# Mixture-of-experts stage: down weights loaded as two or three consecutive rows per partition, and the hidden products written in that order

## The chip, the cores and the metric

One Trainium2 chip, one of its cores. The metric is the device time of one launch in microseconds (us), as the median of the runs. A profiled execution has a time of its own, its span.

## What is computed

The program has three parts: a state-space kernel that makes 256 of the 384 tokens of each of 8 sequences, one attention layer, and a feed-forward layer with 64 experts. The change touches only the last one, here cut to what matters (T = 8 x 384 tokens, 512 wide, 64 experts, hidden width 352, at most 64 tokens for an expert):

```python
g = jnp.einsum('ech,ehi->eci', buf, w_gate)
u = jnp.einsum('ech,ehi->eci', buf, w_up)
y = jnp.einsum('eci,eih->ech', jax.nn.silu(g) * u, w_down)
out_slots = y[flat_i, slot] * (flat_w * valid)[:, None]
...
shared = jax.nn.silu(hidden_states @ sw_gate) * (hidden_states @ sw_up) @ sw_down
return y + shared
```

The last product sums over the 352 hidden values i of an expert. A sum may be taken in any order, so hidden values may stand in any order as long as the rows of `w_down` stand in the same one.

## The kernel before

All 64 experts run in `experts_phase` as 32 pairs (`PAIRS`), two experts of 64 tokens each on the 128 partitions. TensorE (PE) walks through a fixed order for each pair p: it turns the gathered token rows (L1793), multiplies them with the gate and up weights of both experts (L1803, 32 matmuls), turns the products of the hidden layer (`hm`, L1811, three transposes of 128, 128 and 96 columns) and multiplies those with the down weights (L1820, 12 matmuls). Between these four steps there are three gaps for each pair, and in 89 of the 96 gaps PE does a unit of the shared experts: `into_hidden` (L70, 12 matmuls) or `out_of_hidden` (L78, 18 matmuls). Fifteen units make one sequence. The gaps without a unit are gap 2 of pair 7, gap 1 of pair 15, gap 0 of pair 23, gap 2 of pair 30 and all three of pair 31. Gap 1 is the one between gate/up and the transposes of `hm`.

ScalarE (ACT) makes silu of the gate result (L1857). VectorE (DVE) multiplies it by the token's weight and the up result out of PSUM, into `hm` (L1933), copies the turned products back (`hmT`, L1939 and L1940), and copies the rows of y of the second expert (L1946); ACT copies those of the first (L1864). Both keep y in two buffers, and a copy waits until the adds of the pair two before have been done (`added`).

GpSimd (POOL) adds y to the output rows in memory: four indirect DMAs for each pair (L1958), two experts by two halves of the columns. Each waits until the add before it on the same half has landed, since rows may repeat between experts. The shared experts' result of a sequence is added in the same chain (L1966).

The weights come from SyncE (SP) into two sets of buffers, one for even and one for odd pairs. SP waits until gate/up of pair p-2 has been multiplied and issues the four gate and up loads of pair p (L111); then it waits until the down product of pair p-2 is done and issues the down loads of pair p (L118 and L120, two for each expert). A gate or up load takes four consecutive rows per partition, one run of 5,632 bytes. A down load takes rows of 2,048 bytes: chunk c, partition p holds row 128 c + p, and the third chunk has 96 rows. PE waits for all eight loads of a pair before L1803. The first two pairs are loaded by the same functions near the end of the attention part.

Of the kernel before, what the change touches and what calls it, by code (L numbers as in the profile page):

```python
# [11 lines left out]
ALU = mybir.AluOpType  # L12
ACT = mybir.ActivationFunctionType
AX = mybir.AxisListType
P = 128
# [95 lines left out]
            sp.dma_start(place[:, e, g], w[2 * p + e].rearrange("(p k) i -> p k i", p=P)).then_inc(done, 16)  # L111

def load_down(sp, place, w_down, p, done):
    I = w_down.shape[1]
    full = I // P
    for e in range(2):
        sp.dma_start(place[:, e, 0:full, :], w_down[2 * p + e][0:full * P, :].rearrange("(c p) d -> p c d", p=P))\  # L118
            .then_inc(done, 16)
        sp.dma_start(place[0:I - full * P, e, full, :], w_down[2 * p + e][full * P:I, :]).then_inc(done, 16)  # L120

def state_space_phase(nc, x, log_dt, B_ri, inv_A_real, A_imag, ident_in, h_dram, bulk, arena, late,
# [1525 lines left out]
def experts_phase(nc, acc, xrow, x2T_dram, slot_table, w_gate, w_up, w_down, bulk, shared, staged, added,  # L1649
                  late, rows_in, staged1):  # L1650

    E, D, I = w_gate.shape
# [32 lines left out]
    with ExitStack() as ctx:  # L1685
        def sb(name, shape, dt=F32):
            return ctx.enter_context(nc.sbuf_tensor(name, shape, dt))
# [9 lines left out]
        wcol = sb("mo_wcol", [P, 2])  # L1697
        scatter_half = sb("mo_scatter_half", [CAP, 2, E], U32)
        sil = sb("mo_sil", [P, I])
        hm = sb("mo_hm", [P, I])  # L1700
        hmT = sb("mo_hmT", [P, IC, P])
        y = sb("mo_y", [CAP, 2, 2, D])
        ps = ctx.enter_context(nc.psum_tensor("mo_ps", [P, 8, 512], F32))
# [49 lines left out]
        def _(pe):  # L1753
# [33 lines left out]
            for p in range(PAIRS):  # L1787
                j = p % 2
                use = p // 2 + 1
                pe.wait_ge(rows_in[p % 3], 16 * (p // 3 + 1))  # L1790
                wait(pe, rowsT_ready, p)
                for k in range(KC):
                    m = M.transpose(ps[:, 0, k * P:(k + 1) * P], xg[:, p % 3, k:D:KC], ident)  # L1793
                m.then_inc(rows_turned, 1)
                gap(p, 0)

                pe.wait_ge(rowsT_ready, p + 1)
                pe.wait_ge(w_in[j], 16 * 8 * use)
                wait(pe, hidden_ready, p)
                for g in range(2):  # L1800
                    for k in range(KC):
                        for e in range(2):
                            m = M.matmul(ps[CAP * e:CAP * (e + 1), 1 + g, 0:I], xgT[:, k, CAP * e:CAP * (e + 1)],  # L1803
                                         wgu[j][:, e, g, k, :], start=(k == 0), stop=(k == KC - 1))
                m.then_inc(gate_up_done, 1)
                gap(p, 1)

                pe.wait_ge(hidden_ready, p + 1)
                wait(pe, hiddenT_ready, p)
                for c in range(IC):  # L1810
                    m = M.transpose(ps[0:IW[c], 3, c * P:(c + 1) * P], hm[:, c * P:c * P + IW[c]], ident)  # L1811
                m.then_inc(hidden_turned, 1)
                gap(p, 2)

                pe.wait_ge(hiddenT_ready, p + 1)
                wait(pe, ya_ready, p)
                wait(pe, yb_ready, p)
                for c in range(IC):
                    for e in range(2):
                        m = M.matmul(ps[CAP * e:CAP * (e + 1), 4, :], hmT[0:IW[c], c, CAP * e:CAP * (e + 1)],  # L1820
                                     wd[j][0:IW[c], e, c, :], start=(c == 0), stop=(c == IC - 1))
                m.then_inc(down_done, 1)
# [44 lines left out]
        def _(dve):  # L1867
# [54 lines left out]
            for p in range(PAIRS):  # L1922
                j = p % 2
                dve.wait_ge(rows_turned, p + 1)
                wait(dve, gate_up_done, p)
                V.tensor_copy(xgT[:].rearrange("p k t -> p (k t)"), ps[:, 0, :]).then_inc(rowsT_ready, 1)  # L1926
                V.tensor_copy(wcol[0:CAP, j:j + 1], xg[0:CAP, p % 3, D + 2 * p:D + 2 * p + 1])
                V.tensor_copy(wcol[CAP:P, j:j + 1], xg[CAP:P, p % 3, D + 2 * p + 1:D + 2 * p + 2]).then_inc(wcol_ready, 1)
                after_unit(gap_units.get((p, 0)))
                dve.wait_ge(silu_done, p + 1)  # L1930
                dve.wait_ge(wcol_ready, p + 1)
                wait(dve, hidden_turned, p)
                V.scalar_tensor_tensor(out=hm[:], in0=sil[:], scalar=wcol[:, j:j + 1], in1=ps[:, 2, 0:I],  # L1933
                                       op0=ALU.mult, op1=ALU.mult).then_inc(hidden_ready, 1)
                if is_up(gap_units.get((p, 1))):
                    mult_shared(gap_units[p, 1])
                dve.wait_ge(hidden_turned, p + 1)
                wait(dve, down_done, p)
                V.tensor_copy(hmT[:, 0:IC - 1, :], ps[:, 3, 0:(IC - 1) * P].rearrange("p (c t) -> p c t", t=P))  # L1939
                V.tensor_copy(hmT[0:IW[-1], IC - 1, :], ps[0:IW[-1], 3, (IC - 1) * P:IC * P]).then_inc(hiddenT_ready, 1)  # L1940
                after_unit(gap_units.get((p, 1)), multiplied=True)
                after_unit(gap_units.get((p, 2)))
                dve.wait_ge(down_done, p + 1)
                for half in added:
                    wait(dve, half, 16 * (rank["pair", p - 2, 1] + 1) if p >= 2 else 0)
                V.tensor_copy(y[:, j, 1, :], ps[CAP:P, 4, :]).then_inc(yb_ready, 1)  # L1946
# [111 lines left out]
```

## Time and profile before

| | us |
|---|---|
| median of three runs | 1470.59 (1468.84 to 1477.54) |
| span of the profiled execution | 1472.2 |
| PE busy in it | 1291.1 |
| DVE busy | 754.7 |
| ACT busy | 407.8 |
| POOL busy | 499.0 |

The page cuts the span into 40 slices of 36.8 us. The experts' stage begins about 935 us from the start and takes the last 537 us. A line of the timeline is the start of a piece of work, its length, the engine, the line of the kernel and the tiles, and in brackets how long the engine was idle before it and what ended that. A line of the windows is a stretch of time with each engine's busy time and, at its end, the granted TensorE clock, the busy share of the DMA engines and the rate in GB/s.

### The profile page before, as it was taken

Reading aid. Unit: us, or ns where it says so; the run is one execution under the profiler, and the core shown is the slowest. Engines: PE = TensorE matmul, PEld = TensorE weight load, DVE = VectorE, ACT = ScalarE, POOL = GpSimd, SP = SyncE. Lnnn points to the kernel's source line nnn. Section 1 sums busy time; section 2 is a strip of 40 time slices with the busy share of each in tenths; the row PEclk is TensorE's granted clock in tenths of the full one; section 3 lists DMA queues with packets and bytes.
Section 4 is the critical chain, followed back from the end, with each engine's and each line's share of the span. In section 5 each row is a group of like instructions: output and inputs, shape, how many; then the busy total and the mean of one; then the engine's idle time right before and its main releaser. Section 6 shows DMA issues by size and latency. Waiting matters only on the chain. (4 is left out here: it accounts for less than half of the span.)

```text
span 1472.2 us, 23438 instructions
## 1 busy us (share of the span) xinstructions
PE 1291.1 (88%) x9192; PEld 823.0 (56%) x9192; DVE 754.7 (51%) x1666; ACT 407.8 (28%) x671; POOL 499.0 (34%) x453
## 2 busy tenths in 40 slices
PE   5196679999999999989887879999999999999995
PEld 5196434354545464636443668766666666665662
DVE  6984466567676777676765452222232322222321
ACT  2121313334434353444345341111111111111110
POOL 0000101011203434352456366243344444444444
PEclk9598759799999999999999989999999999999997
DMA  3024141221505152523242474699999999898983
GB/s 113 0 61 95 33 96 41 62 63 45 143 23 142 33 151 42 127 65 106 66 135 96 126 258 92 176 297 291 353 309 323 314 342 332 282 354 291 317 278 41
DMA packets 139829, 239.82 MB, mean 163 GB/s; under 512 B 61112, under 2 KB 81224, under 8 KB 139720
## 3 DMA queue, kind: packets, MB, share of 16 engines
q1 hardware_dynamic: 115880, 214.10, 45.6%
q0 software_dynamic: 23840, 24.23, 9.2%
q8 instruction: 73, 1.20, 0.3%
q14 instruction: 36, 0.29, 0.1%
HBM read 175.59 MB, written 38.90 MB: 146 GB/s over the span
## 5 line engine op out<-in xcount | busy, mean ns | idle before, releaser
L1958 POOL DMA_INDIRECT out_rows<-mo_y,mo_scatter_half x128 | 181.1, 1414 | 240.5 <-DMA out_rows<-mo_y,mo_scatter_half 171.6
L1322 DVE TENSOR_REDUCE late_view<-at_ps 128x1 f32<-128x384 f32 x384 | 195.3, 552 | 73.7 <-PE at_ps L893 65.0
L1098 ACT ACTIVATE bulk<-at_ps 128x1152 f32<-128x1152 f32 x128 | 144.6, 1130 | 280.9 <-PE at_ps L859 259.2
L1581 POOL DMA_INDIRECT slot_table<-at_toki,at_si x144 | 144.2, 1001 | 108.9 <-DVE late_view L1322 76.7
L70 PE MATMUL mo_ps<-arena_view,arena_view 128*117 128x384 f32 (+1 forms) x864 | 168.8, 344 | 1.1 <-PEq L549 1.1
L70 PEld LDWEIGHTS mo_ps<-arena_view,arena_view 128*117 128x117 f32 (+1 forms) x864 | 146.5, 179 | 14.6 <-issue 14.5
L893 PE MATMUL at_ps<-late_view 32*128 32x384 bf16 x384 | 102.2, 356 | 27.9 <-DVE late_view L1322 15.8
L850 PE MATMUL at_ps<-arena_view,arena_view 128*128 128x512 f32 (+1 forms) x576 | 115.7, 352 | 3.8 <-ACT arena_view L1176 2.4
L850 PEld LDWEIGHTS at_ps<-arena_view,arena_view 128*128 128x128 f32 x576 | 90.8, 194 | 37.3 <-issue 22.8
L893 PEld LDWEIGHTS at_ps<-late_view 32*128 32x128 bf16 x384 | 28.0, 92 | 142.8 <-DVE late_view L1322 103.4
L859 PE MATMUL at_ps<-arena_view 97*128 97x384 f32 x384 | 99.5, 369 | 8.6 <-DMA arena_view<-late_view 5.1
L1933 DVE SCALAR_TENSOR_TENSOR mo_hm<-mo_sil,mo_wcol,mo_ps 128x352 f32<-128x352 f32 x32 | 18.6, 580 | 155.9 <-ACT mo_sil L1857 141.0
L850 PE MATMUL at_ps<-late_view,late_view 128*128 128x512 f32 x288 | 91.5, 434 | 7.4 <-DVE at_hr L1355 5.3
L1553 POOL TENSOR_TENSOR arena_view<-arena_view,arena_view 128x640 f32<-128x640 f32 x24 | 37.3, 1556 | 173.5 <-DVE arena_view L1307 173.4
L1557 POOL TENSOR_TENSOR late_view<-arena_view,late_view 128x384 fp32r<-128x384 f32 x32 | 32.2, 1016 | 181.4 <-ACT late_view L1155 181.4
L485 PE MATMUL ss_psK<-arena_view,bulk 64*64 64x64 f32 x2048 | 61.9, 222 | 31.7 <-DVE bulk L431 31.7
L878 PE MATMUL at_ps<-bulk,at_ones 128*32 128x384 f32 x768 | 87.7, 531 | 1.2 <-issue 0.9
L878 PE MATMUL at_ps<-bulk,arena_view 128*32 128x384 f32 x768 | 86.2, 524 | 0.0
L859 PEld LDWEIGHTS at_ps<-arena_view 97*128 97x128 f32 x384 | 68.6, 199 | 29.5 <-issue 11.8
L78 PE MATMUL mo_ps<-arena_view,arena_view 117*128 117x512 f32 (+1 forms) x324 | 78.9, 397 | 4.8 <-DVE arena_view L1890 4.8
L1803 PE MATMUL mo_ps<-late_view,mo_xgT 128*64 128x352 f32 x512 | 79.3, 462 | 2.2 <-DVE mo_xgT L1926 2.2
L1803 PE MATMUL mo_ps<-bulk,mo_xgT 128*64 128x352 f32 x512 | 79.3, 462 | 1.1 <-DVE mo_xgT L1926 1.1
(216 smaller groups left out, 1812.0 us busy)
## 6 DMA issues: line engine op xcount, KB each, us to landing
bulk<-in_L_ffn_w_gate SPq DMA_DIRECT2D x32, 704.0 KB
bulk<-in_L_ffn_w_up SPq DMA_DIRECT2D x32, 704.0 KB
late_view<-in_L_ffn_w_gate SPq DMA_DIRECT2D x32, 704.0 KB
late_view<-in_L_ffn_w_up SPq DMA_DIRECT2D x32, 704.0 KB
arena_view<-arena_view SPq DMA_DIRECT2D x96, 192.0 KB
late_view<-in_L_ffn_w_down SPq DMA_DIRECT2D x32, 512.0 KB
bulk<-in_L_ffn_w_down SPq DMA_DIRECT2D x32, 512.0 KB
out_rows<-at_hr SPq DMA_DIRECT2D x8, 768.0 KB, 3.8
```

The source lines that it names most:

```text
L70: m = T.matmul(out, self.gu[:, wa, g, k, self.SO[c]:self.SO[c] + self.SW[c]], self.x2[:, xa, k, :], start=(n == 0), stop=(n == last))
L78: m = T.matmul(out, self.h[0:self.SW[c], xa, c, s * P:(s + 1) * P], self.d[0:self.SW[c], wa, c, :], start=(n == 0), stop=(n == last))
L485: m = T.matmul(psK[half, n % 2, i * STEP:(i + 1) * STEP], Pm[half, k % 2, t, h, :], basis, start=(t == 0), stop=(t == 3))
L850: m = T.matmul(out, xs[:, xa, k, x_cols], ws[:, wa, k, w_cols], start=(n == 0), stop=(n == 3 * KC - 1))
L859: m = T.matmul(ps[:, kt, 0:SEQ], QT[:, NH + h // REP, kt * P:(kt + 1) * P], QT[:, h, :], start=True, stop=True)
L878: m = T.matmul(ps[HD * j:HD * (j + 1), 3 + sums, 0:SEQ], w, PT[:, (REP * G + j) % RING, kt, :], start=(kt == 0), stop=(kt == NT - 1))
L893: T.matmul(ps[:, raw_bank(a, u), 0:SEQ], qb[rows, r, s * P:(s + 1) * P], qb[rows, REP, :], start=True, stop=True).then_inc(raw_scores, 1)
L1098: A.activation(PT[:, N % RING, :, :], ps[:, 0:NT, 0:SEQ], ACT.Exp, scale=float(HD) ** -0.5)\
L1322: V.tensor_reduce(maxes[:, half, s, h:h + 1], ps[:, raw_bank(a, u), 0:SEQ], AX.X, ALU.max, negate=True)\
L1581: G.indirect_dma_start(slot_table, bass.IndirectOffsetOnAxis(ap=si[:, e % 2, m:m + 1], axis=0), toki[:, e % 2, m // TOPK:m // TOPK + 1], N ...
L1803: m = M.matmul(ps[CAP * e:CAP * (e + 1), 1 + g, 0:I], xgT[:, k, CAP * e:CAP * (e + 1)], wgu[j][:, e, g, k, :], start=(k == 0), stop=(k == ...
L1958: G.indirect_dma_start(acc_halves, bass.IndirectOffsetOnAxis(ap=scatter_half[:, half, 2 * p + e:2 * p + e + 1], axis=0), y[:, p % 2, e, co ...
```

## The change

`load_down` gives partitions 0 to 95 three consecutive rows of `w_down` each (rows 3p to 3p+2, one run of 6,144 bytes) and partitions 96 to 127 two rows each (from row 288 on, one run of 4,096 bytes). There are still two loads for each expert, and as many bytes. Hidden value 3p+c then belongs to chunk c, partition p. So that the transposes of `hm` find the values of a chunk side by side, `hm` becomes three blocks of 128 columns, and DVE writes its products in that order, in two instructions: 288 values as 96 by 3 and 64 values as 32 by 2, read in sequence and written with a step of one block (512 bytes). PE and ACT do what they did.

```diff
+def down_rows(I):
+    IC = (I + P - 1) // P
+    wide = I - (IC - 1) * P
+    return IC, wide, IC * wide
 def load_down(sp, place, w_down, p, done):
-    I = w_down.shape[1]
-    full = I // P
+    IC, wide, split = down_rows(w_down.shape[1])
     for e in range(2):
-        sp.dma_start(place[:, e, 0:full, :], w_down[2 * p + e][0:full * P, :].rearrange("(c p) d -> p c d", p=P))\
+        sp.dma_start(place[0:wide, e], w_down[2 * p + e][0:split, :].rearrange("(p c) d -> p c d", c=IC))\
             .then_inc(done, 16)
-        sp.dma_start(place[0:I - full * P, e, full, :], w_down[2 * p + e][full * P:I, :]).then_inc(done, 16)
+        sp.dma_start(place[wide:P, e, 0:IC - 1, :],
+                     w_down[2 * p + e][split:, :].rearrange("(p c) d -> p c d", c=IC - 1)).then_inc(done, 16)
...
-        hm = sb("mo_hm", [P, I])
+        hm = sb("mo_hm", [P, IC, P])
...
-                    m = M.transpose(ps[0:IW[c], 3, c * P:(c + 1) * P], hm[:, c * P:c * P + IW[c]], ident)
+                    m = M.transpose(ps[0:IW[c], 3, c * P:(c + 1) * P], hm[:, c, 0:IW[c]], ident)
...
-                V.scalar_tensor_tensor(out=hm[:], in0=sil[:], scalar=wcol[:, j:j + 1], in1=ps[:, 2, 0:I],
-                                       op0=ALU.mult, op1=ALU.mult).then_inc(hidden_ready, 1)
+                _, wide, split = down_rows(I)
+                for first, last, c, rows in ((0, split, IC, slice(0, wide)), (split, I, IC - 1, slice(wide, P))):
+                    m = V.scalar_tensor_tensor(out=hm[:, 0:c, rows].rearrange("t c p -> t p c"),
+                                               in0=sil[:, first:last].rearrange("t (p c) -> t p c", c=c),
+                                               scalar=wcol[:, j:j + 1],
+                                               in1=ps[:, 2, first:last].rearrange("t (p c) -> t p c", c=c),
+                                               op0=ALU.mult, op1=ALU.mult)
+                m.then_inc(hidden_ready, 1)
```

On SP, in any pair of the stage, these rows stood before (the third number is the shape of one load, partitions first; `bulk` is the buffer of even pairs):

```order
L111 DMA bulk<-in_L_ffn_w_gate 128x1408
L111 DMA bulk<-in_L_ffn_w_up 128x1408
L118 DMA bulk<-in_L_ffn_w_down 128x2x512
L120 DMA bulk<-in_L_ffn_w_down 96x512
L118 DMA bulk<-in_L_ffn_w_down 128x2x512
L120 DMA bulk<-in_L_ffn_w_down 96x512
```

and these stand there now:

```order
L111 DMA bulk<-in_L_ffn_w_gate 128x1408
L111 DMA bulk<-in_L_ffn_w_up 128x1408
L125 DMA bulk<-in_L_ffn_w_down 96x1536
L127 DMA bulk<-in_L_ffn_w_down 32x1024
L125 DMA bulk<-in_L_ffn_w_down 96x1536
L127 DMA bulk<-in_L_ffn_w_down 32x1024
```

No load has moved in the queue; the number stays four, the shapes are other ones.

On DVE, in the pair after the one that ends a sequence, from the copy of the turned token rows to the copy of y, before:

```order
L1926 COPY mo_xgT<-mo_ps 128x512
L1927 COPY mo_wcol<-late_view_51 64x1
L1928 COPY mo_wcol<-late_view_51 64x1
L1933 SCALAR_TENSOR_TENSOR mo_hm<-mo_sil,mo_wcol,mo_ps 128x352
L1882 TENSOR_TENSOR arena_view_63<-arena_view_64,mo_ps 118x384
L1939 COPY mo_hmT<-mo_ps 128x256
L1940 COPY mo_hmT<-mo_ps 96x128
L1890 TENSOR_TENSOR arena_view_59<-arena_view_63,arena_view_59 118x384
L1946 COPY mo_y<-mo_ps 64x512
```

and now (the lines have moved down by 8, and by 14 behind the changed one):

```order
L1934 COPY mo_xgT<-mo_ps 128x512
L1935 COPY mo_wcol<-late_view_51 64x1
L1936 COPY mo_wcol<-late_view_51 64x1
L1943 SCALAR_TENSOR_TENSOR mo_hm<-mo_sil,mo_wcol,mo_ps 128x96x3
L1943 SCALAR_TENSOR_TENSOR mo_hm<-mo_sil,mo_wcol,mo_ps 128x32x2
L1890 TENSOR_TENSOR arena_view_63<-arena_view_64,mo_ps 118x384
L1953 COPY mo_hmT<-mo_ps 128x256
L1954 COPY mo_hmT<-mo_ps 96x128
L1898 TENSOR_TENSOR arena_view_59<-arena_view_63,arena_view_59 118x384
L1960 COPY mo_y<-mo_ps 64x512
```

One instruction has become two at the same place; everything behind it keeps its order.

## Rows read from the trace of the kernel before

**Rows 1.** The page: its head.
```profile
span 1472.2 us, 23438 instructions
```

**Rows 2.** Windows: stretch, its length, busy time of each engine, clock, DMA share, GB/s.
```profile
1375.00:1425.00 50.00, 48.38 (x273) 31.27 (x271) 14.35 (x32) 7.75 (x15) 20.46 (x16) 1.00 1.01 338
1425.00:1472.00 47.00, 29.51 (x146) 14.98 (x142) 7.55 (x17) 2.70 (x5) 22.58 (x16) 0.84 0.41 67
```

**Rows 3.** Waits of PE from 975 us on: us in total, times, longest.
```profile
PE mo_ps L1803 <- DVE mo_xgT L1926: 3.3, 3, 1.4
PE mo_ps L1811 <- DVE mo_hm L1933: 2.4, 2, 1.2
```

**Rows 4.** DMA issues of the even pairs' weights: loads, KB each.
```profile
bulk<-in_L_ffn_w_gate SPq DMA_DIRECT2D x32, 704.0 KB
bulk<-in_L_ffn_w_down SPq DMA_DIRECT2D x32, 512.0 KB
bulk<-in_L_ffn_w_down SPq DMA_DIRECT2D x32, 192.0 KB
```

**Rows 5.** Timeline of one pair around gap 1.
```profile
1204.53 2.34 PE L70 MATMUL mo_ps<-arena_view,arena_view 128*118 128x384 f32 x12
...
1205.14 0.58 DVE L1933 SCALAR_TENSOR_TENSOR mo_hm<-mo_sil,mo_wcol,mo_ps 128x352 f32<-128x352 f32 x1 [6.51 <-ACT mo_sil L1857]
...
1206.71 0.49 PE L1811 MATMUL mo_ps<-late_view,mo_hm 128*128 128x128 f32 x3
```

**Rows 6.** Timeline of PE where gap 1 has no unit.
```profile
1191.56 0.55 PE L1811 MATMUL mo_ps<-late_view,mo_hm 128*128 128x128 f32 x3 [1.18 <-DVE mo_hm L1933]
...
1452.20 0.55 PE L1811 MATMUL mo_ps<-late_view,mo_hm 128*128 128x128 f32 x3 [1.18 <-DVE mo_hm L1933]
```

**Rows 7.** Durations of DVE instructions, by line (mean or min/median/max, ns).
```profile
L1933 DVE SCALAR_TENSOR_TENSOR mo_hm<-mo_sil,mo_wcol,mo_ps 128x352 f32<-128x352 f32 x32 | 18.6, 580 | 155.9 <-ACT mo_sil L1857 141.0 <-issue 14.8
L1939 DVE COPY mo_hmT<-mo_ps 128x256 f32<-128x256 f32 x32 | 13.5, 422 | 42.6 <-PE mo_ps L1811 39.0 <-issue 3.6
L1940 DVE COPY mo_hmT<-mo_ps 96x128 f32<-96x128 f32 x32 | 8.9, 277 | 0.0
...
L351 DVE TENSOR_TENSOR arena_view<-ss_wt x5: 291/292/293, 26.6 to 30.8; 128x128 f32<-128x128 f32 x5
L351 DVE TENSOR_TENSOR late_view<-ss_wt x3: 393/400/402, 32.0 to 37.0; 128x128 f32<-128x128 f32 x3
```

**Rows 8.** Windows near the end: gate/up in flight, down in flight, nothing.
```profile
1419.00:1424.00 5.00, 4.42 (x20) 3.42 (x22) 0.45 (x2) 0.00 (x0) 1.74 (x2) 1.00 1.01 393
1429.00:1432.00 3.00, 3.00 (x15) 2.05 (x16) 0.47 (x1) 0.00 (x0) 1.24 (x1) 1.00 1.05 367
...
1425.20:1427.50 2.30, 2.30 (x14) 1.14 (x11) 0.74 (x2) 0.59 (x1) 1.55 (x2) 1.00 0.00 0
```

**Rows 9.** Chain that ended last: start, us, what; the gate/up of two pairs.
```profile
1395.36 4.88 PE mo_ps L1803 x32
...
1410.48 4.88 PE mo_ps L1803 x32
```

**Rows 10.** Timeline of POOL: adds beside down, beside gate/up, beside down.
```profile
1410.98 1.40 POOL L1958 DMA_INDIRECT out_rows<-mo_y,mo_scatter_half  x1 [4.69 <-DMA out_rows<-mo_y,mo_scatter_half]
...
1417.94 1.40 POOL L1958 DMA_INDIRECT out_rows<-mo_y,mo_scatter_half  x1 [3.85 <-DMA out_rows<-mo_y,mo_scatter_half]
...
1425.64 1.40 POOL L1958 DMA_INDIRECT out_rows<-mo_y,mo_scatter_half  x1 [4.60 <-DMA out_rows<-mo_y,mo_scatter_half]
...
1430.76 1.40 POOL L1958 DMA_INDIRECT out_rows<-mo_y,mo_scatter_half  x1 [2.02 <-DMA out_rows<-mo_y,mo_scatter_half]
```

**Rows 11.** Timeline of DVE and PE: a late copy of y, and waits.
```profile
1310.71 4.95 PE L1803 MATMUL mo_ps<-late_view,mo_xgT 128*64 128x352 f32 x32 [1.38 <-DVE mo_xgT L1926]
...
1325.49 0.69 DVE L1946 COPY mo_y<-mo_ps 64x512 f32<-64x512 f32 x1 [3.29 <-DMA out_rows<-mo_y,mo_scatter_half]
...
1326.96 4.95 PE L1803 MATMUL mo_ps<-bulk,mo_xgT 128*64 128x352 f32 x32 [1.06 <-DVE mo_xgT L1926]
```

## The prediction, made before the changed kernel ran

> **What bounds the kernel now.** I read the span and the windows first. The profiled execution took 1472.2 us [rows 1], 1.6 us more than the median of the runs, 1470.59. In a stretch of 50 us in the experts' stage PE is busy for 48.38 us at the full clock (granted share 1.00, its 2.4 GHz level) and the DMA engines' share is 1.01 at 338 GB/s; only the last 47 us look otherwise [rows 2]. So two resources stand at their limit there, and a change that makes the loads cheaper helps only if PE waits for loads. The waits of PE tell that it doesn't: in 497 us no wait on a DMA stands in that view. It waits 3.3 us for DVE's copy of the token rows and 2.4 us for DVE's products [rows 3]. The chain that ended last runs through PE from one gate/up to the next, 15.12 us for a pair with three L70 units (1410.48 - 1395.36) [rows 9]. Near the end one sees how early weights are: by 1425.2 the DMA engines stand still, so pair 31's gate and up weights have landed [rows 8]; its 4.9 us of products end 1.18 us before the transposes at 1452.20 [rows 6, 9], so they begin at about 1446, 20 us later. Down weights of a pair are issued when the down product two pairs before is done, and are needed at the gate/up of their own pair, more than 15 us later.
>
> There is a third chain, close behind PE: POOL's adds. One round is the adds of one expert. From the timeline: 1410.98 to 1417.94, 6.96 us, with down loads in flight for part of it; 1417.94 to 1425.64, 7.70 us, beside gate/up loads; 1425.64 to 1430.76, 5.12 us, beside down loads and a queue that had been empty [rows 10]. A pair costs POOL 6.96 + 7.70 = 14.66 us, and PE 15.12. The shared adds come on top, the longer pairs with L78 units give it back. Where the chain falls behind, DVE's copy of y waits for an add (3.29 us before the one at 1325.49), DVE is late with the next pair's token rows, and PE stands still: 1.38 us at 1310.71 and 1.06 us at 1326.96 [rows 11]. Those two are 2.44 of the 3.3 us. So loads reach PE's time by way of the adds, not by way of the weights.
>
> **The change part by part.** *Loads.* Their bytes stay: per pair 4 x 704 KB gate/up and 2 x (512 + 192) KB down [rows 4], 2.88 and 1.44 MB. Four issues stay four. Runs of down go from 2 KB (704 for a pair) to 6 and 4 KB (192 plus 64), 448 fewer. With gate/up in flight, runs of 5.6 KB, the rate was 393 GB/s, with down it was 367 [rows 8]. Both windows hold some adds as well, so the gain per pair is at most about 1.44 MB / 367 - 1.44 MB / 393 = 3.92 - 3.66 = 0.26 us, and it lies under PE. The weights were 15 us early: 0 on the path. All the gain could do is to shorten the adds' rounds.
>
> *Products on DVE.* The one instruction takes 580 ns for 352 values. Copies of 256 and 128 values take 422 and 277 ns, 1.13 ns for a value, so a fixed part of 580 - 352 x 1.13 = 182 ns [rows 7]. Two instructions take 182 + 288 x 1.13 = 507 and 182 + 64 x 1.13 = 254 ns. Consecutive DVE instructions overlap by about 80 ns (estimated from L1939 and L1940, which together end 0.62 us after the first began), so 681 ns: 0.10 us more. That is the lower bound. The writes now hop by 512 bytes at each value. No row has this hop; the nearest is L351, which writes 128 single values 32 bytes apart in 400 ns, against 292 ns side by side [rows 7], 0.84 ns more for a value. For 352 values that is 0.30 us, upper bound 0.10 + 0.30 = 0.40 us, which I take, as it is the nearest row. The Trainium skill (Vector Engine (DVE) Microarchitecture Reference, section Measured stream behaviour on trn2) says that a destination which hops at every element costs about 0.65 cycle more per element, at 0.96 GHz an estimate of 0.24 us for 352 values; by it the instructions would cost 0.34 us more. The row with its hop of 32 bytes is somewhat dearer, and the page says the same of small hops.
>
> What hides it: the L70 unit in gap 1. It starts at 1204.53 and runs 2.34 us, the products are ready at 1205.14 + 0.58 = 1205.72, and the transposes start at 1206.71 [rows 5]: 0.99 us of room against 0.40. Behind L1933 on DVE stand the shared product and the two copies of hmT; they wait for PE themselves. In two pairs, 15 and 31, gap 1 is empty, and PE waited 1.18 us in both [rows 6]. There the whole 0.40 us is paid: 0.8 us. PE's transposes read blocks of 128 columns as before, 0.
>
> **Sum.** 1472.2 + 0 (loads) + 0.8 = 1473.0 us for an execution like the profiled one; less the 1.6 us by which it lay above the median, 1471.4 us.
>
> **The rivals.**
> *The adds get shorter.* The saved 0.26 us of DMA time per pair is 1.3 us over the five pairs between two shared adds, and more if the 2 KB runs cost more beside adds than alone. That is the size of the stalls of 1.38 and 1.06 us. If both go: 1471.4 - 2.4 = 1469.0. For it: the margin of 15.12 - 14.66 us is thin. Against: these stalls occur in one of five sequences only, so there is nothing else to win.
> *The adds get longer, and the kernel slower.* An add's rows share the DMA engines with the loads. Beside loads of 5.6 KB a round takes 7.70 us, beside 2 KB loads 5.12 to 6.96 [rows 10]. If an add waits behind a number of runs and not of bytes, the new down loads of 6 KB make the second round as long as the first: 7.70 - 6.96 = 0.74 us more, 15.40 us for a pair, over PE's 15.12. The chain then falls behind by 0.28 us a pair on top of the margin it loses (0.46), so 0.74 x 5 = 3.7 us less is in reserve at the end of each sequence. The sequence with stalls would pay it all, the other four what exceeds their reserve; with 2 us of reserve in these (my estimate from there being no wait now) 3.7 + 4 x 1.7 = 10.5 us, and 1471.4 + 10.5 = 1482. With the 5.12 us round as the measure (7.70 - 5.12 = 2.58 us more a pair, 2.12 of them over the margin) it would be up to 30 x 2.12 = 64 us, 1535; but that round began with an empty queue, and new loads would find it as empty, so I keep it out of the range. It decides from 15.1 us for two rounds. The Trainium skill has the rule (DMA: Bandwidth & Descriptors, section Queues, rings and completion order): an engine goes round the queues by packets and drains some 9 to 17 descriptors of one before it turns to another. Rounds of 7.70 against 6.96 us agree with its direction. Against this rival: down runs go from 44 to 16 for each engine, so hardly more than one such batch is ever ahead, and the batch is 3.7 us at most.
> *Down loads become slow, and weights late.* Now two thirds of the partitions (0 to 63 of 96) take most of the first transfer, and the second one goes to 32 partitions. 
>
> **How the numbers follow.** Forecast, with or without a gain for the DMA engines, 0.60; shorter adds 0.22; longer adds 0.12; slow down loads 0.03; something else 0.03. About 1% (14.7 us) is what a measurement of this kernel can tell from no change. Within it lie the forecast, the shorter adds and over half of the longer adds; slower by more: 0.05 + 0.03 + 0.01; faster by more needs a gain that no wait of PE offers, 0.02. The forecast's own range is 1470.6 (DVE at its lower bound, 0.2 us: 1470.8, and a little less) to 1473. The range of 8 in 10 reaches down to the shorter adds less the runs' own scatter (the lowest run was 1.8 us under the median), 1467, and up into the longer adds, 1480; the highest run of before, 1477.54, lies inside.
>
> **What would show it.** Right: L1943 as 64 instructions, the two of a pair together about 1.0 us; PE's wait before the transposes of pairs 15 and 31 about 1.6 instead of 1.18 us, and in no other pair; no wait of PE on a DMA; a similar or lower DMA share at the same PE time; fewer packets on the page, by about 14,300. The adds decide the rest: two rounds of POOL well under 14.7 us and no wait at the places of 1310.71 and 1326.96 speak for the shorter adds; rounds beside down near 7.7 us, more waits of ACT's and DVE's copies of y on an add, and waits of PE on the token rows in each sequence speak for the longer ones. Wrong would be: PE waiting before L1811 for anything but DVE (weights late), or the products so slow that the 0.99 us of gap 1 is used up, which would need more than 1.6 us for the two.

## The result, and the profile after

The changed kernel takes 1512.72 us (median of 5 runs, 1507.5 to 1521.89) against 1470.59 us for the kernel before (5 runs, 1467.23 to 1477.54). The ratio is 1.0268 with a 95% interval of 1.0231 to 1.0306: 2.7% slower, far outside the predicted range. (Ratios here and below are taken over undisturbed executions alone, so they can differ a little from the quotient of two medians; the profiled execution of e5, with 1521.98 us the longest of its six, is not among them.)

The head of the page of after, and the waits of PE from 975 us on (in total, times, longest). The lines of before stand 8 to 14 further down: gate/up L1803 is now L1811, the transposes L1811 are L1819, DVE's products L1933 are L1943, the copy of the token rows L1926 is L1934, DVE's copy of y L1946 is L1960, the pair adds L1958 are L1972.

```profile
span 1520.0 us, 23470 instructions
PE 1291.4 (85%) x9192; PEld 823.4 (54%) x9192; DVE 766.0 (50%) x1698; ACT 407.9 (27%) x671; POOL 501.3 (33%) x453
PE mo_ps L1811 <- DVE mo_xgT L1934: 52.0, 7, 13.3
PE mo_ps L1819 <- DVE mo_hm L1943: 2.9, 2, 1.5
```

Against [rows 1, 3] PE waits 48.7 us more for DVE's copy of the token rows and 0.5 us more for the products. It still waits for no DMA of weights. The experts' stage runs from the first gate/up to the end: 1472.2 - 940.05 = 532.2 us before and 1520.0 - 931.63 = 588.4 us after.

```profile
940.05 4.95 PE L1803 MATMUL mo_ps<-bulk,mo_xgT 128*64 128x352 f32 x32
```
```profile
931.63 4.95 PE L1811 MATMUL mo_ps<-bulk,mo_xgT 128*64 128x352 f32 x32
```

(The stage happened to start 8.4 us earlier in this execution; in the kernels below the start of the stage moves by some 10 us, without order.) Of the 56.2 us, 49.2 are those waits. The rest is PE's clock. Behind each of the four long stalls (10.16, 13.29, 13.12 and 11.22 us) the granted share falls from 1.00, its 2.4 GHz level, to the 1.2 GHz one for a while. The windows (stretch, length, busy time of PE, PEld, DVE, ACT, POOL, granted clock, DMA share, GB/s) that hold a long stall show it below 1, the ones between at 1:

```profile
1125.00:1175.00 50.00, 39.84 (x212) 25.21 (x210) 12.02 (x28) 5.63 (x11) 23.58 (x18) 0.90 0.81 235
1175.00:1225.00 50.00, 46.08 (x255) 29.49 (x251) 12.76 (x27) 7.05 (x12) 13.94 (x10) 1.00 1.05 310
1225.00:1275.00 50.00, 39.18 (x216) 24.56 (x217) 13.00 (x30) 6.14 (x12) 22.27 (x17) 0.86 0.88 252
```

The timeline of PE shows a gate/up group behind a stall and the next one. The first runs at a lower clock for part of its time, 2.2 us longer. The four groups behind the four stalls lose 2.2, 1.7, 1.6 and 2.9 us, 8.3 together. Before had lost 1.7 us in the same way at its very last down product, which after doesn't, so 7 us remain.

```profile
1139.19 7.16 PE L1811 MATMUL mo_ps<-bulk,mo_xgT 128*64 128x352 f32 x32 [10.16 <-DVE mo_xgT L1934]
...
1156.53 4.95 PE L1811 MATMUL mo_ps<-late_view,mo_xgT 128*64 128x352 f32 x32
```

**What is late.** The waits of all engines name it:

```profile
DVE mo_y L1960 <- DMA out_rows<-mo_y,mo_scatter_half: 75.0, 7, 17.9
POOL out_rows L1972 <- DMA out_rows<-arena_view: 58.7, 10, 10.2
```

Before, these were

```profile
DVE mo_y L1946 <- DMA out_rows<-mo_y,mo_scatter_half: 10.9, 6, 3.3
POOL out_rows L1958 <- DMA out_rows<-arena_view: 29.3, 10, 4.5
```

In time order, one stall on POOL, DVE and PE:

```profile
1207.96 1.52 POOL L1972 DMA_INDIRECT out_rows<-mo_y,mo_scatter_half  x1 [10.19 <-DMA out_rows<-arena_view]
1216.26 1.46 POOL L1972 DMA_INDIRECT out_rows<-mo_y,mo_scatter_half  x1 [6.78 <-DMA out_rows<-arena_view]
```
```profile
1234.35 0.69 DVE L1960 COPY mo_y<-mo_ps 64x512 f32<-64x512 f32 x1 [17.94 <-DMA out_rows<-mo_y,mo_scatter_half]
1235.08 0.69 DVE L1934 COPY mo_xgT<-mo_ps 128x512 f32<-128x512 f32 x1
```
```profile
1235.82 4.56 PE L1811 MATMUL mo_ps<-late_view,mo_xgT 128*64 128x352 f32 x18 [13.29 <-DVE mo_xgT L1934]
```

The two adds of the shared rows hold POOL's chain for 17 us, the pair adds behind them are late, DVE's copy of y may not overwrite its buffer for 17.94 us, the copy of the next token rows stands behind it, and PE has nothing to multiply. That is the chain of [rows 11], with a wait of PE ten times as long. It comes in each sequence: in the first PE waits only 1.07 and 2.28 us, in the four others 10 to 13. The rounds of the pair adds in one pair picked as in [rows 10] are:

```profile
1371.10 1.42 POOL L1972 DMA_INDIRECT out_rows<-mo_y,mo_scatter_half  x1 [6.15 <-DMA out_rows<-mo_y,mo_scatter_half]
...
1378.64 1.39 POOL L1972 DMA_INDIRECT out_rows<-mo_y,mo_scatter_half  x1 [4.43 <-DMA out_rows<-mo_y,mo_scatter_half]
...
1388.95 1.42 POOL L1972 DMA_INDIRECT out_rows<-mo_y,mo_scatter_half  x1 [5.91 <-DMA out_rows<-mo_y,mo_scatter_half]
```

7.54 us beside gate/up as before, but 10.31 us beside the new down loads, 17.85 us for this pair against 14.66 before and PE's 15.12. (Means over the stage follow behind the table.)

**Why the adds are late.** A stretch of 3 us in which only down loads and adds are in flight, as the 367 GB/s of [rows 8], and the landing times of the page, which stand at the end of an issue's row:

```profile
1399.50:1402.50 3.00, 3.00 (x21) 1.61 (x21) 1.11 (x2) 0.52 (x1) 0.19 (x1) 1.00 1.08 301
1478.00:1481.00 3.00, 3.00 (x16) 2.13 (x16) 0.31 (x1) 0.00 (x0) 0.66 (x1) 1.00 1.03 299
...
bulk<-in_L_ffn_w_gate SPq DMA_DIRECT2D x32, 704.0 KB, 7.4
bulk<-in_L_ffn_w_down SPq DMA_DIRECT2D x32, 576.0 KB, 7.8
```

The DMA engines are as taken as before and move 300 instead of 367 GB/s: 1.44 MB take 4.8 instead of 3.9 us, 0.9 us more for a pair. Counted over every microsecond of the stage in which no gate/up load was in flight and down loads took most of the engines' time, the mean rate is 314 GB/s before and 258 after. A transfer of 576 KB lands 7.8 us after its issue, one of 704 KB for gate after 7.4. The packets' own durations in the trace say the same (medians): 84 ns for 2 KB before; after, 378 ns for 6 KB and 264 ns for 4 KB. The 5.6 KB packets of gate/up stay at 215. The loads of the shared experts' turned token rows (x2T below) come in 6 KB packets over 128 partitions, and those took 234 in before. So it is not the length of a run that is slow. Which transfers are, the experiments asked.

### The profile page after: what moved, and what is told of

Same layout as the page of the kernel before. It is cut to its first block and busy times, and to the rows that moved or that the text cites. A ratio compares the mean times of both kernels' runs of the same rounds, so it can differ in the third digit from the quotient of the medians.

```text
span 1520.0 us, 23470 instructions
## 1 busy us (share of the span) xinstructions
PE 1291.4 (85%) x9192; PEld 823.4 (54%) x9192; DVE 766.0 (50%) x1698; ACT 407.9 (27%) x671; POOL 501.3 (33%) x453
## 2 busy tenths in 40 slices
DMA packets 125493, 239.82 MB, mean 158 GB/s; under 512 B 61112, under 2 KB 81224, under 8 KB 125384
## 5 line engine op out<-in xcount | busy, mean ns | idle before, releaser
L1972 POOL DMA_INDIRECT out_rows<-mo_y,mo_scatter_half x128 | 182.3, 1424 | 297.0 <-DMA out_rows<-mo_y,mo_scatter_half 198.7
L70 PEld LDWEIGHTS mo_ps<-arena_view,arena_view 128*117 128x117 f32 (+1 forms) x864 | 146.5, 179 | 14.6 <-issue 14.5
L901 PE MATMUL at_ps<-late_view 32*128 32x384 bf16 x384 | 102.2, 353 | 27.9 <-DVE late_view L1330 15.4
L1943 DVE SCALAR_TENSOR_TENSOR mo_hm<-mo_sil,mo_wcol,mo_ps 128x288 f32<-128x288 f32 x64 | 28.2, 522 | 164.3 <-ACT mo_sil L1865 164.3
L1811 PE MATMUL mo_ps<-late_view,mo_xgT 128*64 128x352 f32 x512 | 82.5, 477 | 28.3 <-DVE mo_xgT L1934 28.3
L1811 PE MATMUL mo_ps<-bulk,mo_xgT 128*64 128x352 f32 x512 | 84.4, 485 | 23.7 <-DVE mo_xgT L1934 23.7
L886 PE MATMUL at_ps<-bulk,at_ones 128*32 128x384 f32 x768 | 84.6, 519 | 0.4 <-DVE late_view L1330 0.4
L1960 DVE COPY mo_y<-mo_ps 64x512 f32<-64x512 f32 x32 | 22.2, 693 | 122.4 <-DMA out_rows<-mo_y,mo_scatter_half 75.0
```

The source lines that it names most:

```text
L70: m = T.matmul(out, self.gu[:, wa, g, k, self.SO[c]:self.SO[c] + self.SW[c]], self.x2[:, xa, k, :], start=(n == 0), stop=(n == last))
L886: m = T.matmul(ps[HD * j:HD * (j + 1), 3 + sums, 0:SEQ], w, PT[:, (REP * G + j) % RING, kt, :], start=(kt == 0), stop=(kt == NT - 1))
L901: T.matmul(ps[:, raw_bank(a, u), 0:SEQ], qb[rows, r, s * P:(s + 1) * P], qb[rows, REP, :], start=True, stop=True).then_inc(raw_scores, 1)
L1972: G.indirect_dma_start(acc_halves, bass.IndirectOffsetOnAxis(ap=scatter_half[:, half, 2 * p + e:2 * p + e + 1], axis=0), y[:, p % 2, e, co ...
```

## The experiments

Three readings stand in the table at the end of this section, for the runs that differ in their loads. *Down time* and *add* are read from the one profiled execution of each run. *Ratio* is to the kernel before on the same chip. *Down time* is the sum of all durations of packets of 2, 4 and 6 KB behind 940 us over 16 engines (x2T's 640 packets included; for e10, all packets less the 220 us that gate and up take in before). *Add* is the time from the end of a pair add's issue to the last of its 16 semaphore increments, the means of the two halves of the columns summed, over the 44 to 57 adds of each half that can be told apart. (Over all such adds behind 940 us before has 9.09 and after 10.37; a choice of adds moves an entry by up to 0.25.)

**The loads or the products?** e1 takes after's `load_down` into before, e2 does the reverse.

> The down loads of after with VectorE's and TensorE's code of before; the hidden units then meet other rows of the down weights, so the part of the computation that is changed is which row each product is multiplied with, not how much work is done. Theory A (the loads of after slow the adds): 1511 to 1513 us, TensorE waits of 10 to 13 us for xgT once per sequence as in after, sum near 50 us. Theory B (VectorE's two strided products are what costs): 1470 to 1472 us.

> VectorE's products and the transposes of after with the loads of before (again other rows meet; no work is left out). Theory A: 1470.6 to 1471.4 us, that is up to 0.8 us over before, as the 0.3 us longer pair of products is on the path only in the two pairs with an empty first gap. Theory B: about 1512 us.

Measured: ratios 1.0247 (1.0180 to 1.0313) and 1.0019 (0.9979 to 1.0059). PE's waits from 975 us on:

```profile
PE mo_ps L1811 <- DVE mo_xgT L1934: 5.1, 3, 3.5
...
PE mo_ps L1819 <- DVE mo_hm L1943: 2.9, 2, 1.5
```

This is e2. It has the 0.5 us that the products cost, and one wait of 3.5 us for the token rows, with gate/up behind it 2.7 us longer at a lower clock; nothing of after's 52.0 us. In e1 the wait for the token rows is

```profile
PE mo_ps L1811 <- DVE mo_xgT L1934: 41.6, 7, 12.2
```

Theory A holds: the loads are the cause.

**Length of runs, or partitions?** e3 gives after's shape to runs of 2 KB, e4 gives 4 KB runs to all 128 partitions:

```diff
# e3: load_down of after with
-  .rearrange("(p c) d -> p c d", c=IC)
+  .rearrange("(c p) d -> p c d", c=IC)
# e4: load_down of before with
-  w_down[2 * p + e][0:full * P, :].rearrange("(c p) d -> p c d", p=P)
+  w_down[2 * p + e][0:full * P, :].rearrange("(p c) d -> p c d", p=P)
```

> The shape of after's transfers (96 partitions with three rows, then 32 with two) but each row its own run of 2 KB, 22,528 packets of 2 KB as before; VectorE and TensorE as before (other rows meet, no work is left out). Theory P (the uneven spread over partitions is what slows the down loads and, through them, the adds): about as slow as after, 1500 to 1515 us. Theory R (the length of the runs does it): as before, 1469 to 1473 us. Both together: between.

> Runs of 4 KB over all 128 partitions (rows 0 to 255 two by two), the last 96 rows in runs of 2 KB as before, and VectorE writing its products in that order; the result is the reference's. Theory P: down packets of 4 KB take some 165 ns (twice the 84 ns of 2 KB), the adds keep their 5 us, 1469 to 1472 us. Theory R: 4 KB packets hold the adds up in part, 1480 to 1500 us.

Measured: e3 1.0215 (1.0164 to 1.0266), e4 1.0008 (0.9967 to 1.0049). In stretches with down loads and adds alone, e3 and then e4:

```profile
1393.50:1396.50 3.00, 3.00 (x20) 1.57 (x21) 1.11 (x2) 0.52 (x1) 0.37 (x1) 1.00 1.09 305
```
```profile
1062.50:1065.50 3.00, 3.00 (x22) 1.29 (x18) 0.08 (x1) 0.00 (x0) 2.39 (x3) 1.00 1.04 358
```

Runs as short as before are slow in the new shape, 134 ns for 2 KB instead of 84. Runs twice as long over 128 partitions are not (164 ns for 4 KB). e4's profiled execution, 1483.0 us and the third longest of its ten, does have stalls, a third of after's:

```profile
PE mo_ps L1803 <- DVE mo_xgT L1926: 15.6, 6, 8.7
```

So before's kind of kernel is close to its edge too, and single executions cross it; the median of ten is that of before. Most of the loss goes with how the rows are dealt out to partitions, and theory R falls as the main cause.

e4 shows one thing more. Its only 2 KB packets are those of the third chunk, one row in each of 96 partitions, and their median is 84 ns (131 at the upper tenth). So 96 partitions with one row each are not slow; 96 with three rows each, followed by 32 with two, are.

**Near 128 partitions.** e5 gives three rows to 117 partitions and one row to one more; e9 three rows to 112 partitions and one row to each of the last 16; e10 takes the 704 KB as one transfer of 128 partitions with one run each.

```diff
# e5 (e9 with n = 112; its rest goes to place[n:P, e, 0, :])
+        sp.dma_start(place[0:n, e], w_down[2 * p + e][0:3 * n, :].rearrange("(p c) d -> p c d", c=3))...
+        sp.dma_start(place[n:n + 1, e, 0:1, :], w_down[2 * p + e][3 * n:I, :]...)
# e10
+        flat = w_down[2 * p + e].rearrange("i d -> (i d)").rearrange("(p k) -> p k", p=P)
+        sp.dma_start(place[:, e].rearrange("p c d -> p (c d)")[:, 0:I * D // P], flat)...
```

> The longest runs on evenly used partitions: 117 partitions with three rows each (6 KB), one more partition with the last row, and VectorE's products in that order (the second instruction has one column); the result is the reference's. Theory P (uneven spread): 6 KB packets take some 235 ns as those of x2T over 128 partitions did in the trace of before, the adds keep 3 to 6 us, 1469 to 1474 us. Theory R (run length): packets near 370 ns, adds of 7 to 8 us beside down, 1500 to 1515 us.

> As the run with 117 partitions, but 112 partitions with three rows each (6 KB; 112 is 16 x 7) and the last 16 rows one by one in the partitions 112 to 127; the result is the reference's. Theory E (what counts is the time of the busiest DMA engine, and 117 partitions gave work to 13 of 16 engines only): 6 KB packets take 235 to 300 ns, down takes some 150 us of engine time per engine over the stage instead of 180, and the time is 1470 to 1485 us. Theory R (runs of 6 KB hold the adds up whatever their spread): 1500 to 1515 us.

> The same 704 KB for each expert as one transfer of 128 partitions with one run of 5.6 KB each, as gate and up come (two down transfers for a pair instead of four; the pieces of rows then meet other products, no matrix product is left out). Theory E: packets of 215 to 230 ns, engine time of down at its least, about 110 us over the stage, adds no slower than beside gate/up, 1467 to 1472 us. Theory R, which is the forecast's own rival (an add waits behind a number of runs): both rounds of a pair 7.7 us, 15.4 against PE's 15.12, 1480 to 1485 us or more.

Measured: e5 1.0171 (1.0113 to 1.0229), e9 1.0206 (1.0111 to 1.0300), e10 1.0007 (0.9969 to 1.0045). I had expected e5 and then e9 to be nearly as fast as before (1469 to 1474 and 1470 to 1485 us), and both were not: their medians are 1513.17 us over all six executions and 1504.68. The packets of e5 are nearer to those over 128 partitions (median 260 ns against 234), but fewer engines carry them: the semaphores of its weight loads show 1,342 and 1,407 increments behind 960 us against 1,792 and 1,874 in after, which is what 13 engines would give (13 for the large transfer, 1 for the small, and 2 written at the issues, in place of 32). Its down time of 146.5 us over 16 engines is thus 180 over 13. The adds look alike: the first increment comes 2.9 and 2.6 us after the issue, earlier than in before (3.6 and 3.3), but the last one another 2.4 us later (1.1 in before), as it would be with three engines free of down loads and thirteen not. The Trainium skill (DMA: Bandwidth & Descriptors, section Why a DMA increments its semaphore by 16 and not by 1) has that rule: as many engines as the largest number up to 16 that divides the slowest dimension, for 117 it is 13. The increments agree.

e9 uses 16 engines, and its 6 KB packets still take 356 ns in the median. So 112 partitions are hardly better than 96. The Trainium skill (SBUF — State Buffer, section Door 1: The DMA port swizzle) counts the ports that a range of partitions reaches, and 112 partitions reach all 16 by its table, as do 96. By that count alone neither should be slow; the runs show that both are. e10 is the control: 128 partitions, one run of 5.6 KB each, packets at 215 ns, and the time of before. It also ends the forecast's own rival, in which an add waits behind a number of runs: all loads of a pair were then of the kind beside which a round took 7.70 us, the two rounds took 14.5 us on the mean and not 15.4, and PE's wait was

```profile
PE mo_ps L1801 <- DVE mo_xgT L1924: 6.9, 3, 3.9
```

And it shows what a faster down load could win: the down time falls from 148 to 124 us, and the kernel gains nothing, because PE is at its limit.

**By way of the adds?** e6 is after with four buffers of y (the copies wait for the adds of the pair four before), e7 is after without the adds of the shared rows in this stage.

> The kernel after with four buffers of y instead of two, so that the copies of y wait for the adds of the pair four before. If the adds fall behind in bursts only, around each shared add, the stalls go and the time is 1472 to 1480 us. If the chain of adds is too long as a whole (about 9.7 + 7.5 = 17.2 us for a pair against PE's 15.12), the buffers only move the stall to the end: PE's waits for xgT shrink, but the last adds are later after the last product, and the time is 1490 to 1512 us.

> The kernel after without the six adds of the shared experts' rows in the experts' stage (that part of the output is left out; the products that make the rows are still computed, and the add before the stage stays). If the stalls come by way of the chain of adds, which these lengthen by some 17 us in each sequence: PE's waits for xgT fall from 52 to under 8 us and the time to 1471 to 1475 us, with down packets as slow as in after. If the slow down loads reach PE in another way (weights late, SBUF ports): 1500 us or more.

Measured: e7 0.9986 (0.9946 to 1.0025), with 52.0 us of waits down to 1.7, although its down loads are as slow as after's (375 ns).

```profile
PE mo_ps L1809 <- DVE mo_xgT L1933: 1.7, 2, 0.8
```

So the slow loads reach PE only through the chain of adds. e6 1.0228 (1.0178 to 1.0278), 1503 us. Its waits of PE, from 975 us on:

```profile
PE mo_ps L1801 <- DMA late_view<-rows_scores,late_view: 26.7, 3, 13.1
...
PE mo_ps L1811 <- DVE mo_xgT L1934: 1.7, 2, 0.8
```

With more buffers DVE no longer waits, but the gathers of the token rows stand on POOL's queue behind the adds and come late instead. The adds also end later: from PE's last product to the end it takes 21.9 us, 14.3 in after. The chain, shared adds included, is too long as a whole, not only in bursts; buffers move the wait.

**How much of it?** e8 gives after's transfers to the first expert of each pair only.

> Half the dose: the kernel before with the down weights of one expert of each pair in after's transfers, the other's as before (rows of the first expert meet other products, no work is left out). If the loss is in proportion to the slow transfers: 1490 to 1493 us. If there is a margin that has to be used up first: 1471 to 1482 us. A pair's two rounds would take some 15.9 us (midway between 14.66 and 17.2) against PE's 15.12, so I expect the first or a little under it.

Measured 1.0193 (1.0134 to 1.0252): half the dose costs 0.7 of the loss (1.93% of 2.68%). The expert left as before is hit too: its 2 KB packets take 116 instead of 84 ns in the median.

**Engine time alone?** e11 and e12 are before with two or one more loads of 256 KB for each pair, over all partitions:

```diff
+                for e in range(2):   # e12: range(1)
+                    sp.dma_start(spare[:, j, e, :], w_down[2 * p + e][0:P, :]).then_inc(w_in[j], 16)
                 load_down(sp, wd[j], w_down, p, w_in[j])
```

> The kernel before, unchanged in its loads and products, with two more loads of 256 KB for each pair (the first 128 rows of each expert's down weights once more, to a place that nobody reads, over all 128 partitions in runs of 2 KB). They add 256 packets of 84 ns to 16 engines, 1.3 us for a pair or some 40 us over the stage, so the down loads with them take about 188 us of each engine's time where before took 148 and after 178. Theory T (what counts is the time for which the DMA engines are taken, however it comes about): about 1500 to 1512 us, with the waits for xgT of after. Theory U (an add is held up by the single slow packets of badly spread transfers, not by the engines being taken): 1470 to 1478 us.

> The same with one more load for each pair: 128 packets, 0.67 us for a pair, about 168 us of engine time in all. Theory T: near the run with one expert's weights in after's transfers (173 us of engine time, 1496 us), so 1482 to 1496 us. Theory U: 1470 to 1474 us.

Measured: 1.0108 (1.0076 to 1.0140) and 1.0071 (1.0036 to 1.0106). The same stalls appear without one badly spread transfer more; e11's wait for the token rows:

```profile
PE mo_ps L1806 <- DVE mo_xgT L1929: 25.4, 6, 10.1
```

So the engines' time is part of the cause, and theory U falls as the whole. But 189 us of down time cost 1.1% here, and 178 in after 2.7%. Theory T falls as the whole, too.

**Where does the rest come from?** Either the adds' reads of y, which lies in partitions 0 to 63, compete with the crowded transfer, or the bad spread itself delays an add. e13 mirrors both transfers (three rows to partitions 32 to 127), e14 mirrors those of the second expert only, e15 moves the second expert's y to partitions 64 to 127, and e16 does that in before.

> The kernel after with its two transfers of each expert mirrored: three rows each to partitions 32 to 127, two rows each to partitions 0 to 31 (the third product of the down step then reads the second chunk of the weights again; it does the same work on other rows, so that part of the result is changed). Theory Y (the adds' own reads of y in partitions 0 to 63 compete with the crowded transfer, which went to partitions 0 to 95): the crowd moves away from y in two thirds of the bytes, 1485 to 1500 us. Theory S (the spread of a transfer over the engines alone, wherever y lies): as after, 1507 to 1515 us.

> The same mirrored for the second expert of each pair only, so that the engines and partitions that one expert crowds are the free ones of the other (again the third product reads the second chunk's weights). Theory S, if the backlog of one engine over both experts matters: 1485 to 1500 us. If each transfer is slow by itself and nothing evens out: 1507 to 1515 us. Theory Y: between after and the mirrored run.

> The kernel after with the second expert's y in partitions 64 to 127 instead of 0 to 63 (the result is the reference's). Theory Y: the rounds of the second expert's adds get shorter, 1490 to 1503 us. Theory S: no change, 1508 to 1515 us.

> The kernel before with the second expert's y in partitions 64 to 127 (the result is the reference's). Theory Y: the few stalls left, 3.3 us in the profile of before, go: 1467 to 1471 us. Theory S: 1470 to 1472 us. The difference is too small to tell them apart; the run is there as a possible better version.

Measured: e13 1.0239 (1.0195 to 1.0283), e14 1.0296 (1.0259 to 1.0334), e15 1.0268 (1.0214 to 1.0322), e16 0.9993 (0.9954 to 1.0032). None helps. Theory Y falls: within what these runs can tell, it doesn't matter where y lies or which end is crowded. Evening the crowd out between the experts doesn't help either; each such transfer is slow by itself. e16 is no better version, and with e4 and e10 at no change I know of none.

The runs in order of the add's time:

| run | down loads (partitions x rows) | ratio | down time, us | add, us |
|---|---|---|---|---|
| e10 | 128, one run | 1.0007 | 124 | 8.94 |
| before | 128 x 2, 96 x 1 | 1 | 148 | 9.18 |
| e4 | 128 x 2 (4 KB), 96 x 1 | 1.0008 | 142 | 9.26 |
| e12 | before and one more | 1.0071 | 167 | 9.62 |
| e11 | before and two more | 1.0108 | 189 | 9.80 |
| e8 | after's and before's | 1.0193 | 173 | 10.10 |
| e3 | 96 x 3, 32 x 2, 2 KB runs | 1.0215 | 186 | 10.16 |
| e9 | 112 x 3, 16 x 1 | 1.0206 | 170 | 10.33 |
| e5 | 117 x 3, 1 x 1 | 1.0171 | 146 (180 over 13) | 10.46 |
| e1 | 96 x 3, 32 x 2 | 1.0247 | 175 | 10.47 |
| e14 | one expert mirrored | 1.0296 | 180 | 10.49 |
| after | 96 x 3, 32 x 2 | 1.0268 | 178 | 10.54 |
| e13 | mirrored | 1.0239 | 173 | 10.65 |

The ratio goes with the last column in three groups: up to 9.26 us there is no loss, at 9.62 and 9.80 it is 0.7 and 1.1%, above 10.1 it is 1.7 to 3.0%, without order inside the group. The down time sorts them less well.

**From the adds to the loss.** The halves run beside each other, so a round holds one of the two times. Where an add started as soon as the one before it on its half had landed, two rounds took 14.3 us on the mean in before (76 starts) and 16.1 in after (81) and in e7 (72). PE's own work takes 16.1 us for a pair on the mean, the pairs with L78 units included: 940.05 to its last product at 1457.95, less the 3.3 us of waits, over 32 pairs. A shared add holds a half for 9.2 us before and for 12.6 us after, from its own start to the start of the next add. The 15 units of one sequence take some 5.4 pairs. In that time before has 5.4 x 1.8 = 9.7 us in hand for the 9.2 of the shared add; after has nothing in hand for 12.6. Its four long stalls are 10.2 to 13.3 us. In e7 the pair rounds are as long as in after and just fit, so without the shared adds nothing is lost. For e11 (15.1 us for a pair, 12.3 for a shared add) the same sum gives 7 us in each of four sequences, 29 us in all; its waits were 25.4. This sum is an estimate from means, but it says why a chain with a margin before has none after, and why neither the pair rounds nor the shared adds alone explain the loss.

## Why the prediction was wrong

*What bounds the kernel*: right. PE's time for a pair, the DMA engines' share of 1, and the chain of adds close behind PE were the three things that mattered; no weights came late. The margin of 0.46 us came from one pair; on the mean over the stage it was 1.8 us, and the shared adds used nearly all of it.

*Loads cost 0*: this step failed. It put 393 against 367 GB/s and read the difference as what longer runs would win, 0.26 us for a pair. The rate fell to 300 GB/s, 0.9 us for a pair the other way, and two rounds of adds grew by 1.8 us (14.3 to 16.1). The comparison had changed two things at once: gate/up has long runs, but also 128 partitions in every transfer. The trace of before gave no warning: its own loads of 96 partitions, with one row each, were not slow (84 ns for the same chunk in e4). It took three rows in each of them, a shape that none of its down loads had.

*The rivals*: the truth was the path of one with the cause of another. "The adds get longer" named the chain, the threshold (two rounds over 15.1 us) and every sign to look for, but priced the rounds at 15.40 from a wrong cause, runs counted instead of bytes; they are 17.85 in the pair shown above, 16.1 on the mean, where before had 14.3. It was then 1482 instead of 1513 us, and had 0.12. "Down loads become slow" named the cause, the spread over partitions, with 0.03, but let it act by late weights, where 15 us of lead had to be used up. Two arguments were put against it. That the old third chunk had 96 partitions too is true, but it proved nothing for three rows in each of them (e3 against e4). That two transfers in flight fill both halves didn't help: not even mirrored ones did (e14). I never let the slow loads act on the adds, although the prediction itself says that "loads reach PE's time by way of the adds, not by way of the weights".

*Reserve*: I took 2 us for four of the five sequences and left the shared adds as they were. They too share the engines: they hold a half for 12.6 us where it was 9.2, and the chain without them has no long stall at all (e7). The reserve was not 2 us left over but 9.7 us for the 9.2 of a shared add, and it was gone once the pair rounds had grown.

*Products on DVE*: right in place and nearly in size. The group of L1943 and one pair of them:

```profile
L1943 DVE SCALAR_TENSOR_TENSOR mo_hm<-mo_sil,mo_wcol,mo_ps 128x288 f32<-128x288 f32 x64 | 28.2, 522 | 164.3 <-ACT mo_sil L1865 164.3
```
```profile
1198.39 0.85 DVE L1943 SCALAR_TENSOR_TENSOR mo_hm<-mo_sil,mo_wcol,mo_ps 128x288 f32<-128x288 f32 x2 [6.55 <-ACT mo_sil L1865]
1199.30 0.55 PE L1819 MATMUL mo_ps<-late_view,mo_hm 128*128 128x128 f32 x3 [1.45 <-DVE mo_hm L1943]
```

The two take 0.85 us together (0.90 in another pair), 0.27 to 0.32 more than 0.58 where I took 0.40. PE's wait grows from 1.18 to 1.45 and 1.46 us in the two pairs with an empty gap 1, and in no other, 0.5 us in all where I had 0.8. e2 agrees, as far as its 1.0019 can tell.

*Packets*: 125,493 on the page against 139,829, 14,336 fewer, as worked out.

*The range*: the range's upper end, 1480, cut off both rivals just where their causes meet. The case that I kept out of it, rounds that take 2.12 us over the margin, up to 1535, was nearer than the one I kept.

*The clock*: not foreseen. Each of the four long stalls cost PE 1.6 to 2.9 us of lower clock behind it; against before, 7 us on top of 49. A wait need not be that long: behind e2's one of 3.5 us gate/up took 7.62 instead of 4.95 us.

## What to carry to other kernels

A DMA's shape is part of its cost. Loads of two or three rows each into 32, 96 or 112 partitions took 1.5 to 1.6 times as long for each packet as loads into all 128; 117 partitions took 1.1 times as long, but on 13 engines. That weighed more than whether a run had 2, 4 or 6 KB. A single row in each of 96 partitions, on the other hand, cost nothing, so measure the shape that you mean to use. When two rates from a trace are compared, first list everything in which the two transfers differ. And when a resource at its limit feeds a chain with little margin, price a change by what it does to that chain, even where the thing that is loaded comes early itself.

## What the runs showed of the hardware

- Packets of transfers over 128 partitions took 84, 164, 215 and 234 ns in the median for 2, 4, 5.6 and 6 KB, some 24 to 26 bytes in a nanosecond for each engine. Three rows each in 112 or 96 partitions: 6 KB took 356 and 378 ns, and as single rows 2 KB took 134 (e3). Two rows each in 32 partitions: 4 KB took 264. One row each in 96 partitions: 2 KB took 84 (e4). Joining runs of 2 KB to 4 or 5.6 KB over 128 partitions gained this kernel nothing (e4, e10).
- At no more engine time, badly spread transfers delay an add more than well spread ones: 10.16 to 10.54 us against 9.80. Against before, most of it is in the wait for the first of the 16 increments (after 4.08 and 3.74 us, e11 3.89 and 3.65, before 3.62 and 3.34). Against e11, whose engines are as busy, the larger part is in the spread from the first to the last (1.33 and 1.40 us, e11 1.17 and 1.08). Why such a transfer is slow, why one row in each of 96 partitions is not, and what holds the add up beyond the engines' time stays open: the packet records don't name their engine.
- Others in flight are slowed too: beside such transfers 2 KB packets of the old shape took 116 instead of 84 ns in the median (e8).
